# The middle state's sum of squares in the guess moves: on ScalarE instead of VectorE

## The reference

```python
def rms(z):
    return z / jnp.sqrt(jnp.mean(z * z, axis=-1, keepdims=True) + EPS)

O_lh = polar_orthogonal(W_lh)      # 12 iterations X <- 1.5 X - 0.5 X X^T X
O_rh = polar_orthogonal(W_rh)
q, v = x @ Wq, x @ Wv
def step(h, q_t):
    h_new = rms(h @ O_lh.T + q_t @ O_rh.T)
    return (h_new, h_new)
Y = (qs * v) @ Wc                  # qs: all states h
# ffn: sqrt((x @ cos(theta + noise))**2 + (x @ sin(phi + noise))**2)
```

## Time and profile before

| | us |
|---|---|
| median of 3 runs (140.16 to 141.63) | 140.2 |
| time of the profiled execution | 140.24 |
| its span, first to last instruction | 138.4 |
| busy in the span: PE 116.6, DVE 103.2, ACT 76.4, POOL 55.1 | |

### The profile page before, as it was taken

One profiled execution on the slowest core, in us unless ns is written; L12 is line 12 of the kernel. 1 busy time (PEld: TensorE's weight loads), 2 busy tenths in 40 slices (PEclk: granted clock), 3 DMA queues, 4 the chain that ended last, 5 costly groups with the idle time before them and its releaser, 6 DMA issues.

```text
span 138.4 us, 2697 instructions
## 1 busy us (share of the span) xinstructions
PE 116.6 (84%) x775; PEld 91.5 (66%) x775; DVE 103.2 (75%) x411; ACT 76.4 (55%) x284; POOL 55.1 (40%) x92
## 2 busy tenths in 40 slices
PE   6988898789999999999999967788878888788861
PEld 6766777689966666666666644577756767577740
DVE  3579999984476777777777777578887877878862
ACT  4035999997546666666556566643534334353430
POOL 7302786850024444445555544553232322323220
PEclk9999999999999999999999999999999999999999
DMA  4884000000000000000000000001020220202211
GB/s 123 236 247 174 0 0 7 0 0 0 5 0 2 0 0 0 0 5 0 0 0 0 5 0 0 2 5 69 7 76 0 81 76 2 76 0 81 76 38 40
DMA packets 3342, 4.95 MB, mean 36 GB/s; under 512 B 448, under 2 KB 1344, under 8 KB 3328
## 3 DMA queue, kind: packets, MB, share of 16 engines
q1 hardware_dynamic: 3024, 4.46, 9.9%
q0 software_dynamic: 160, 0.26, 0.7%
q10 hardware_dynamic: 144, 0.07, 0.2%
HBM read 2.69 MB, written 2.10 MB: 35 GB/s over the span
## 4 chain that ended last, share of the span: by engine, by line
PE 45%; DVE 39%; ACT 6%; issue 6%; DVEq 1%; POOL 0%
DVE W L679 8%; PE bank L947 7%; DVE SQM L665 7%; PE bank L906 7%; PE bank L938 5%; DVE VT L702 5%; PE bank L954 4%; DVE WMID L660 4%; PE bank L862 4%; DVE WTM L686 3%; DVE bank L673 3%; PE bank L846 3%; PE bank L957 2%; PE bank L790 2%; PE bank L785 2%
## 5 line engine op out<-in xcount | busy, mean ns | idle before, releaser
L293 POOL TENSOR_TENSOR FS<-FSQ 128x256 f32<-128x256 f32 x16 | 11.6, 724 | 36.9 <-ACT FSQ L423 36.9
L906 PE MATMUL bank<-IDENT,W 128*128 128x128 f32 x31 | 10.1, 327 | 11.2 <-DVE W L679 11.1
L408 ACT ACTIVATE SQE<-W 128x129 f32<-128x129 f32 x32 | 10.0, 313 | 15.6 <-DVE W L679 15.6
L286 POOL TENSOR_SCALAR XN<-X,MV,RSTD 128x128 f32<-128x128 f32 x16 | 13.5, 847 | 11.8 <-DVE RSTD L563 11.8
L906 PEld LDWEIGHTS bank<-IDENT,W 128*128 128x128 f32 x31 | 4.3, 139 | 19.6 <-DVE W L679 19.6
L929 PE MATMUL bank<-CS,XNT 128*128 128x256 f32 x64 | 16.5, 380 | 0.0
L790 PE MATMUL bank<-ONES 128*128 128x128 bf16 x158 | 16.1, 219 | 0.0
L640 DVE COPY WT<-bank 128x128 f32<-128x128 f32 x30 | 8.7, 292 | 9.2 <-PE bank L906 9.2
L947 PE MATMUL bank<-WCT,PV 128*128 128x128 f32 x64 | 14.6, 310 | 0.7 <-POOL PV L317 0.6
L954 PE MATMUL bank<-PXT,WT 128*128 128x128 f32 x60 | 14.6, 325 | 0.0
L317 POOL TENSOR_TENSOR PV<-VT,WTM 128x128 f32<-128x128 f32 x16 | 7.3, 453 | 18.3 <-DVE WTM L686 18.3
(11 more groups left out here) (170 smaller groups left out, 286.7 us busy)
## 6 DMA issues: line engine op xcount, KB each, us to landing
X<-in_L_attn_x_dram SPq DMA_DIRECT2D x8, 256.0 KB, 6.9
out_dram<-OUT SPq DMA_DIRECT2D x7, 256.0 KB, 2.0
out_dram<-OUT SPq DMA_DIRECT2D x2, 128.0 KB, 1.7
WP<-in_L_attn_W_rh_dram ACTq DMA_DIRECT2D x1, 64.0 KB, 1.9
WP<-in_L_attn_W_lh_dram SPq DMA_DIRECT2D x1, 64.0 KB, 2.2
ANG<-in_L_ffn_theta_dram POOLq DMA_DIRECT2D x1, 64.0 KB, 3.5
WV<-in_L_attn_Wv_dram SPq DMA_DIRECT2D x1, 64.0 KB, 3.3
ANG<-in_L_ffn_phi_dram POOLq DMA_DIRECT2D x1, 64.0 KB, 3.2
```

The source lines that it names most:

```text
L286: pool.tensor_scalar(XN[:, t, :], X[:, t, :], MV[:, t, 0:1], RSTD[:, t:t + 1], ALU.subtract, ALU.mult).then_inc(S["xn_pool"], 1)
L293: pool.tensor_tensor(FS[:, f % 2, :, :], FSQ[:, f % 2, :, 0:P], FSQ[:, f % 2, :, P:2 * P], ALU.add).then_inc(S["ffn_sum"], 1)
L906: pe.transpose(TB[:, 0:P], W[:, 0:P], IDENT[:, :]).then_inc(t_done, 1)
```

## The change

In `act` the branch on `m < GUESSES` goes: ACT takes the sum of squares of `WMID` in all 32 moves, by the two lines that the final moves had. In `dve` the function `mid_norm` and its one call are taken out. Nothing else is edited; the semaphore `ssm_ready` is now raised by ACT alone.

```diff
--- before.py
+++ after.py
@@ -433,12 +433,9 @@
                 pair_copied(q)
             for m in range(LAST):
                 j = MOVES[m]
-                if m < GUESSES:
-                    act.wait_ge(ssm_ready, m + 1)
-                else:
-                    act.wait_ge(mid_ready, m + 1)
-                    act.activation(SQM[:, 0:E], WMID[:, 0:E], ACT.Square, accum_out=SSM[:, 0:1]).then_inc(ssm_ready, 1)
-                    act.wait_ge(ssm_ready, m + 1)
+                act.wait_ge(mid_ready, m + 1)
+                act.activation(SQM[:, 0:E], WMID[:, 0:E], ACT.Square, accum_out=SSM[:, 0:1]).then_inc(ssm_ready, 1)
+                act.wait_ge(ssm_ready, m + 1)
                 act.activation(RT[:, j:j + 1], SSM[:, 0:1], ACT.Sqrt, scale=1.0 / C).then_inc(rm_ready, 1)
                 norm_of_state(m + 1)
                 if m + AHEAD < GUESSES:
@@ -660,12 +657,6 @@
                 dve.scalar_tensor_tensor(out=WMID[:, 0:E], in0=UZ[:, uz(j), 0:E], scalar=norm_of(m),
                                          in1=YB[:, 0:E], op0=ALU.mult, op1=ALU.add).then_inc(mid_ready, 1)
 
-            def mid_norm(m):
-                dve.wait_ge(mid_ready, m + 1)
-                dve.tensor_tensor_reduce(out=SQM[:, 0:E], in0=WMID[:, 0:E], in1=WMID[:, 0:E], scale=1.0,
-                                         scalar=0.0, op0=ALU.mult, op1=ALU.add,
-                                         accum_out=SSM[:, 0:1]).then_inc(ssm_ready, 1)
-
             def second(m, j):
                 if m == 0:
                     dve.wait_ge(S["uz_copied"], 1)
@@ -708,7 +699,6 @@
                 if m:
                     v_copied(m - 1)
                 mid(m, j)
-                mid_norm(m)
                 second(m, j)
                 end(m, j)
                 transposed(m + 1)
```

## The result

| | us |
|---|---|
| before, median of 4 runs (140.16 to 141.63) | 140.69 |
| changed, median of 4 runs (135.71 to 136.24) | 135.83 |
| ratio, with its 95% interval | 0.965 [0.959, 0.972] |
| profiled execution: before 140.24, changed | 136.24 |

What follows compares the result with a forecast made beforehand. The prediction took one serial loop through several engines as the bound, with DVE's pass held by POOL. From 140.2 us, -4.2 - 0.16 + 0.25 + 0.10 = -4.0 gave 136.2 us, range 135.7 to 137.5.

Steps and rivals of the forecast that it cites:

- The pass of DVE is held by POOL's `FS`: Guess moves: DVE's sum of squares waits inside itself until POOL's ffn sum ends, median 710 ns against a minimum of 294.
- A guess move takes 2.86: Moves m=2 to 14: 1.74 from W to WMID plus 1.12 to W, instead of 3.185; times 13, -4.2 us.
- ACT has 0.04 us of slack, PE 0.07: Guess moves: ACT is free 0.04 us before the Square is due, PE 0.07 before the transpose is due.
- both late rivals: Guess moves: Square waits for FR to drain, 137.6 us, chance 0.09; transpose waits for ffn matmuls' end, 137.4, chance 0.06.
- The terms of single moves: Outside the 13 moves: m=0 costs +0.25 us, m=1 gives -0.16, m=15 costs +0.10.
- POOL's durations unchanged: Guess moves, POOL: a listed sign that its instructions keep the durations they had before the change.
- The final moves and what lies ahead of m=0 keep their own time: Outside the guess moves: final moves keep their own distances; the sum has no term for them or for the start.
- The time of 137.5: Estimate by the Trainium skill's page: 0.41 us for the Square of 129 elements, about 0.22 saved a move, about 137.5 us.

Runs made afterwards that it cites:

- e1: Kernel before, with one wait added on POOL so that the ffn sum FS never runs beside DVE's pass: 134.73 us, ratio 0.955 to before.
- e3: Kernel before, with WMID also formed in PSUM in the guess moves and DVE's pass reading one operand from there: 138.74 us, one run.
- e5: Kernel before, with POOL's ffn sum FS cut into two instructions of 128x128: 137.04 us, one run.
- e7: Changed kernel, with one more one-element root on ACT behind FR in guess moves from m=1: 137.56 us, one run.
- e6: Changed kernel, with four small filler matmuls on PE ahead of each ffn in the guess moves: 138.47 us, one run.
- e9: The kernel of e1 run again as it is: 134.86 us.
- e10: The kernel of e1 with 16 one-column memsets added on DVE at the start: 134.89 us.
- e2: The changed kernel run again as it is: 136.07 us, ratio 0.965 to before.
- e4: Changed kernel, but DVE takes the sum of squares as before in m=0 and m=15: 136.57 us against 136.07 for the changed kernel.
- e8: Changed kernel with 16 one-column memsets added on DVE at the start: 136.98 us, one run.

## Why the prediction was right

The forecast was 136.2 us in 135.7 to 137.5, and the median is 135.83. Step by step:

- *The pass of DVE is held by POOL's `FS`.* Shown, by e1 (POOL moved away, 0.71 falls to 0.30), e3 (one operand elsewhere, 0.29) and e5 (POOL's instruction halved, 0.44). It was argued before from three coincidences in time.
- *A guess move takes 2.86.* It takes 2.867; 13 moves gave 4.14 instead of 4.2, which is the rounding of 1.74 and 1.12. The chain of the changed kernel, in order of time, no longer runs from `WMID` to the Square but along ACT's own queue:

```profile
60.35 0.50 ACT FSQ L423
60.85 0.30 ACT FR L430
61.15 0.35 ACT SQM L437 x2
```

It reads as if the Square waited for `FR`, and it doesn't. The Square starts before `FR` has ended, so ACT is never idle there and the chain stays on it. But it starts 0.385 after `WMID`, and 0.382 to 0.386 after it in the final moves of the same profile, where no `FR` is ahead (m=20 below); and e7 found 0.045 us of slack:

```profile
95.90 0.35 DVE L657 SCALAR_TENSOR_TENSOR WMID<-UZ,RT,bank 128x129 f32<-128x129 f32 x1
...
96.29 0.31 ACT L437 ACTIVATE SQM<-WMID 128x129 f32<-128x129 f32 x1 [1.08 <-DVE WMID L657]
```

- *ACT has 0.04 us of slack, PE 0.07.* e7 says 0.045, e6 says 0.09. So both late rivals were near, and neither held. That the two engines could start early, behind an instruction that had not ended, was read from m=0 and holds in every move.
- *The terms of single moves*, +0.25, -0.16 and +0.10, came out as +0.26, -0.15 and +0.10 (from `W` of m=14 to `W` of m=15: 2.81, now 2.90; `WMID` to `W`: 1.02, now 1.12). The 0.25 was a slip in the subtraction, 40.09 - 39.83 is 0.26. Together with the 13 moves: -3.94, where the forecast had -4.0.
- *POOL's durations unchanged.* Right for `FS` (0.72 and 0.73), not for `XF`: its median fell from 0.773 to 0.724 us. In e1, where DVE's pass never runs beside POOL, it is 0.72 too, so beside the pass POOL had been held a little as well.
- *The final moves and what lies ahead of m=0 keep their own time.* This was wrong twice, with opposite signs. The final moves lost the stop above, -0.35. And m=0 began later in both profiles of the changed kernel (37.01 and 36.94 against 36.47). The difference arises in the first 8 us, on PE. Timeline of PE, the changed kernel and then before:

```profile
4.67 1.06 PE L775 MATMUL bank<-ONES 128*128 128x128 f32 x4
5.52 1.06 PE L836 MATMUL bank<-PX 128*128 128x128 f32 x4
6.71 0.90 PE L852 MATMUL bank<-PP,PXT 128*128 128x128 f32 x4
```

```profile
4.67 0.69 PE L785 MATMUL bank<-ONES 128*128 128x128 f32 x4
5.34 0.71 PE L846 MATMUL bank<-PX 128*128 128x128 f32 x4
```

The same four filler matmuls at 4.67 take 1.06 us in the changed kernel and 0.69 before; the next ones lose as much. In both kernels PE has run such matmuls almost without a pause since 1.20. They start every 0.21 us at first and every 0.11 later, which are the lower and the higher of the two levels of PE's clock (1.2 and 2.4 GHz), and the higher comes at about 4.8 us before and at about 7.2 in the changed kernel. The trace's own record of the granted clock begins at just these times, with 1.00. What the views print for the time ahead of it is 1.00 too, for want of a record; so they, and the "full throughout" of the profile before, say nothing of the first microseconds.

PE's instructions up to there are the same in all runs. The record begins between 4.1 and 6.3 us in the six profiles without the change (before, e1, e3, e5, e9, e10) and between 4.5 and 7.4 in the six with it (changed, e2, e4, e6, e7, e8), so a late rise occurs without the change (e10, 6.3) and an early one with it (e4, 4.5). Since five of the six with it are at 6.2 or later, a part of the change in it isn't excluded; that stays open. e4 and e9 begin m=0 late (36.91 and 36.78) for another reason: at 8.1 us PE waits 0.58 for the landing of `WQ`, a load from memory.

The profiled execution with this loss is the slowest of its four (136.24 against 135.71 to 135.92). That it meets the forecast of 136.2 so exactly is luck: the guess moves gave -3.94 by the mechanism, and +0.54, -0.38 and -0.16 around them, which were not in the sum, cancel. Without the late clock it would have been 135.7 by an estimate from the same table, which is where the others are.

The time of 137.5, which the prediction worked out from the Trainium skill ("ScalarE: Activation LUTs", Rules for kernel authors), did not come true: the Square has 0.31 us in the guess moves too, and lets the next instruction in 0.22 after it began. The prediction had also left out that row's condition: the Trainium skill gives its 0.3 us for an ACTIVATE whose bias is a pointer operand, and the kernel gives the Square no bias.

What I had not seen is the better remedy. The prediction found the cause and did not ask what a wait on POOL would give. By the same numbers, an undisturbed DVE pass gives 1.02 from `WMID` to `W` against ACT's 1.12, and one wait on an idle POOL is enough for it: 134.7 to 134.9 us in e1 and e9. There PE sets the move: it is busy in 35.92 of 35.99 us, and 2.867 less the 0.09 that e6 found free is 2.78. So no more is to be had from `WMID` to `W`.

## What to carry to other kernels

When an operation has one duration beside an idle neighbour and more than twice that beside a busy one, look for the instruction of another engine that ends just before it does, before moving the operation elsewhere: delaying or splitting the neighbour may be cheaper. A move to another engine pays that engine's own price, also in the places where nothing was in the way. And a gain of 0.3 us in a total can be outweighed by a stop that the edit has only shifted; read it from the stretch that was edited.

## What the runs showed of the hardware that was not expected

- DVE's pass with two SBUF operands, when it comes during a POOL operation on SBUF, has its readout 0.09 us after that operation's end, and gets its turn between two queued POOL instructions (e5).
- DVE can stop for 0.34 to 0.41 us at a place in its stream, with nothing in the profile that it waits for (before, e1, e3, e4, e5, e9). In e10 and e3, with 16 instructions more ahead of it, the stop of 0.34 at m=25 is gone and 0.12 is lost at m=24.
- PE's step from the lower to the higher level of its clock came at 4.1 to 7.4 us in the twelve profiles, under the same matmuls, and this moved the start of m=0 by half a microsecond (36.47 and 37.01).
- In some executions PE's granted clock falls for a while as the final moves begin. In e1, the stretch 82 to 86 us:

```profile
82.00:86.00 4.00, 3.41 (x20) 2.68 (x19) 2.46 (x9) 1.95 (x9) 2.96 (x5) 0.62 0.03 6
```

The last but two number is the granted clock, 0.62 as a mean of the stretch; from 83 to 86 us it is 0.50, the lower level. Until 76.86 PE had been busy in nearly all of the guess moves (35.92 of 35.99 us, above). From `W` of m=16 to `W` of m=17 it took 3.66 us there, and 2.94 in the profile before. e7 and e8 show the same in their single runs (3.64 and 3.57), so 0.7 us of their totals is this; e9, with e1's kernel and the same load (35.91 of 35.98 us), keeps 1.00 and has 2.93. e1's profiled execution took 135.43, its others 134.48 to 134.92. So a single run should not be read to better than that.
